# Mixture-of-experts layers of a two-layer decoder: two token lists in separate expert tiles, or in shared ones

## The chip, the cores and the metric

The kernel runs on one core of a Trainium2 chip, as one launch. The metric is the device time of that launch in microseconds, the median of several runs. The profiled executions are single ones, taken by the hardware profiler.

## The reference

A pre-layernorm decoder of two layers over x of 64 x 64 tokens (4096) of width 128, all in fp32. Each layer adds to x a sequence mixer, a cross-attention over a context of 64 tokens, and a feed-forward part with 8 routed experts (128 to 512 to 128), of which each token uses 2:

```python
# layer 0: sigmoid gate, two shared experts, exact gelu
balanced = sigmoid(x @ centroids.T + routing_bias)
_, top_idx = top_k(balanced, 2)
top_w = softmax(take_along_axis(sigmoid(raw), top_idx, -1), -1)
h_r = gelu(einsum('bsd,efd->bsef', x, Wfc_r)); expert_out = einsum('bsef,edf->bsed', h_r, Wproj_r)
return x + shared_out + einsum('bsed,bse->bsd', expert_out, combine)
# layer 1: softmax gate, biases, tanh gelu
topk_scores, topk_idx = top_k(softmax(x @ Wg + bg), 2)
for e in range(8):
    output = output + (gelu(x @ W1[e] + b1[e]) @ W2[e] + b2[e]) * combine_w[..., e:e + 1]
```

The change touches these two parts alone.

## The kernel before

The program is a row of phases: state-space mixer, attention, `ffn0`, retention, attention, `ffn1`. Both feed-forward phases are `ffn_phase` with other settings. The names below are those of its code.

**Routing.** The 4096 tokens are 32 token tiles of 128, in 8 groups of 4. DVE normalizes x (`xn`), TensorE makes the gate's logits, and DVE turns them into one-hots of the first and second expert. Two products (`prefix`) give, for each token, how many tokens of its tile stand before it at its expert, and each tile's count by expert. From these a chain of DVE instructions, each of which waits for the one before (`seq`), works out for every token and choice a slot: a place in a list ordered by expert and padded so that each expert begins a new *expert tile* of 128 slots.

**Two lists.** The token tiles are cut in two parts of 20 and 12 (`part_tiles`). Each part has its own list with its own padding: 2 x 20 x 128 + 8 x 127 slots cut to whole tiles is 47 expert tiles, and 31 for the second. These are fixed lengths, so M = 78 tiles are computed whatever the routing is. The first list is ready sooner, so that the tiles can start; the one-hots of the last three groups (`hot`) are made inside the loop at steps 4, 10 and 16.

**From slot to token.** `hot` makes, for a group, one-hots of the slot's row and of its tile; `collect` multiplies them on TensorE (16 products with 47 or 31 columns), and the sum in PSUM is the token of each slot. `sources` copies it to `source`. In `ffn1` POOL makes one of the two multiplications of `hot` for the first five groups (`BY_POOL`). The expert of each tile (`owner`) comes from eight DVE instructions on one partition, four for each list.

**The tile loop.** For each tile POOL gathers 128 rows of `xn` by an indirect DMA; TensorE transposes them, DVE copies the transpose, ACT copies the expert's up weights, TensorE makes 4 up products (8 instructions), ACT the gelu (with DVE's bias before it in `ffn1`), TensorE 4 down products (8 instructions), DVE copies the result out, and SP stores each two tiles to DRAM (`slots_y`). Step s transposes tile s, does the up products of tile s - 2 and the down products of tile s - 4. POOL issues the gathers in lots of up to 4 tiles; a lot waits until TensorE has transposed a tile that is 8 to 20 before its end (`AHEAD_FIRST`, `AHEAD_MORE`).

**Back to tokens.** After the last lot POOL gathers, for each group, the two result rows of each token: 8 indirect DMAs a group. Groups 0 to 4 wait for the first list's stores, 5 to 7 for all. The rows go to two buffers (those of `hot_row`), so the turn for group m waits until DVE has added group m - 2 to x (`add_rows`). DVE adds group 0 from step 72 on in `ffn0`, groups 0 and 1 from steps 66 and 72 in `ffn1`, a quarter in each step, and the others after the loop.

**Around the loops.** In `ffn0` two shared experts work on all tokens in 16 units on TensorE: 6 units before the loop, with `prefix` and the `collect`s between them, 10 after it. In `ffn1` there are none. TensorE fills the waits with transposes whose result nobody reads (`warm`: 28 at the phase's start, 88 after `prefix`, 6 after each `collect`, 24 more).

Of the kernel before, what the change touches and what calls it, by code (L numbers as in the profile page):

```python
# [19 lines left out]
F32 = mybir.dt.float32  # L20
# [3 lines left out]
ALU = mybir.AluOpType  # L24
# [1403 lines left out]
def ffn_phase(g, name, spec):  # L1428
# [6 lines left out]
    parts, E, PM = len(part_tiles), E0 + EXPERTS, max(part_tiles)  # L1435
    V = parts * EXPERTS
    counts = [slot_tiles(t) for t in part_tiles]
    M, NM = sum(counts), max(counts)
    start = [sum(counts[:part]) for part in range(parts + 1)]
    first_tile = [sum(part_tiles[:part]) for part in range(parts + 1)]  # L1440
    first_group = [t // GTILES for t in first_tile]
    part_of = [part for part in range(parts) for _ in range(counts[part])]
    RING = TILES
    BY_POOL, ADDED_AT = range(first_group[1]) if spec["last"] else (), spec["added_at"]
    lots = [(start[part] + begin, size) for part in range(parts)
            for begin, size in in_lots(counts[part], (1, 1, 2, 4) if part == 0 else (4,))]
    lot_of = {begin: n for n, (begin, _) in enumerate(lots)}
    stores = [(part, begin, size) for part in range(parts) for begin, size in in_lots(counts[part], (STORED,))]
    store_of = {start[part] + begin + t: n for n, (part, begin, size) in enumerate(stores) for t in range(size)}
    stores_of = [sum(1 for part, _, _ in stores if part < upto) for upto in range(parts + 1)]  # L1450
    with ExitStack() as ctx:
# [12 lines left out]
        if biased:  # L1464
# [3 lines left out]
        slots_y = [nc.dram_tensor(f"{name}_slots_y{part}", (counts[part] * P, D), F32,  # L1468
                                  kind="Internal").ap() for part in range(parts)]

        by_token, by_expert = [P, TILES, EXPERTS], [P, V, PM]
# [13 lines left out]
        tile_starts, tile_numbers = sb("tile_starts", [P, TILES]), sb("tile_numbers", [P, NM])  # L1485
# [4 lines left out]
        ones_row, per_tile, running, over = (lent(k, by_expert) for k in ("ones_row", "per_tile", "running", "over"))  # L1490
        earlier, count, tiles = sb("earlier", [P, V]), sb("count", [P, V]), sb("tiles", [P, V])
        tile_end, offset = sb("tile_end", [P, V]), sb("offset", [P, V])
        ended, tile_owner = lent("ended", [1, NM, EXPERTS]), sb("tile_owner", [1, NM])
# [76 lines left out]
        with nc.Block() as block:  # L1570
# [26 lines left out]
            def _(pool):  # L1597
# [28 lines left out]
                for m in range(GROUPS):  # L1626
                    part = max(p for p in range(parts) if first_group[p] <= m)
                    if m in first_group:
                        stores_done(pool, stores_of[part + 1])
# [10 lines left out]
            def _(dve):  # L1640
# [127 lines left out]
                for q in range(first_group[1]):  # L1768
                    hot(q)
# [326 lines left out]
```

## Time and profile before

| | us |
|---|---|
| median of 3 runs | 1282.48 |
| the three runs | 1277.87, 1282.48, 1283.58 |
| profiled execution, whole | 1278.75 |
| its span, first to last instruction | 1277.0 |
| TensorE matmuls busy | 1135.2 (89%) |
| DVE busy | 830.1 (65%) |
| ACT busy | 652.2 (51%) |
| POOL busy | 611.2 (48%) |
| mean granted TensorE clock | 0.95 |

Times in the profile count from the first instruction. `ffn0` runs from 208 to 516 us, its loop from 284.7 to 441.1; `ffn1` from 1008 to the end, its loop from 1064.1 to 1223.9. PE is TensorE, PEld its weight loads, DVE VectorE, ACT ScalarE, POOL GpSimd, SP the engine that issues plain DMAs. In a timeline a row says when a run of like instructions starts, how long it takes, how many they are, and in brackets how long the engine had been idle before it and what ended that. The end of a row is its start plus its length.

### The profile page before, as it was taken

The numbers are of one execution on the slowest core, as the hardware profiler recorded it, in microseconds if no ns is written. First come the engines' busy times: TensorE is split into PE (matmuls) and PEld (weight loads), VectorE is DVE, ScalarE is ACT, GpSimd is POOL, SyncE is SP. The second block draws the span as 40 slices with busy tenths as digits, with TensorE's granted clock in tenths as the row PEclk, the third lists the DMA queues.
The fourth block names the chain that finished last, engine by engine and source line by source line (L and its number), as shares of the span: only waits on it lengthen the run. The fifth ranks groups of instructions, "written<-read, shape, count | busy, mean of one in ns | idle before, by whom it ended". The sixth has DMA issues, their size and how long they took to land. (4 is left out here: it accounts for less than half of the span.)

```text
span 1277.0 us, 31999 instructions
## 1 busy us (share of the span) xinstructions
PE 1135.2 (89%) x11702; PEld 959.3 (75%) x11702; DVE 830.1 (65%) x1800; ACT 652.2 (51%) x1171; POOL 611.2 (48%) x627
## 2 busy tenths in 40 slices
PE   6979997999999999399999999987899878999930
PEld 4766666689999877288888888875577778999930
DVE  6868997743222343378888888884689675666742
ACT  5417774425566542166665665653687503566610
POOL 4761325126567474733334444333254326566775
PEclk9999999899999999699999999998999888999975
DMA  7001213202233321100000000000110331233332
GB/s 193 10 2 49 54 49 136 102 17 65 71 77 82 98 71 32 39 2 1 0 0 0 1 0 0 0 1 6 21 19 17 113 109 44 68 79 78 87 108 64
DMA packets 61908, 62.64 MB, mean 49 GB/s; under 512 B 12592, under 2 KB 50864, under 8 KB 61296
## 3 DMA queue, kind: packets, MB, share of 16 engines
q1 hardware_dynamic: 51824, 42.52, 11.2%
q0 software_dynamic: 9088, 18.63, 6.3%
q8 instruction: 62, 1.02, 0.3%
q14 instruction: 38, 0.31, 0.1%
q10 hardware_dynamic: 896, 0.17, 0.1%
HBM read 42.67 MB, written 16.52 MB: 46 GB/s over the span
## 5 line engine op out<-in xcount | busy, mean ns | idle before, releaser
L1623 POOL DMA_INDIRECT f_xn<-f_xn_rows,f_source x156 | 149.0, 955 | 49.4 <-issue 48.2
L1977 PE MATMUL f_bank<-f_xT,f_w_tile 128*128 128x128 f32 x1248 | 167.5, 278 | 0.0
L1988 PE MATMUL f_bank<-f_w_down,f_hidden 128*128 x1248 | 165.1, 276 | 0.0
L1977 PEld LDWEIGHTS f_bank<-f_xT,f_w_tile 128*128 128x128 f32 x1248 | 154.4, 195 | 0.0
L1988 PEld LDWEIGHTS f_bank<-f_w_down,f_hidden 128*128 128x128 f32 x1248 | 152.5, 193 | 0.0
L1634 POOL DMA_INDIRECT f_hot_row<-f_slots_y,f_slots x128 | 123.7, 966 | 38.3 <-issue 38.0
L1050 POOL TENSOR_TENSOR ret_rstd<-ret_var,ret_minus_half 128x8 f32<-128x8 f32 x32 | 52.7, 1647 | 173.8 <-DVE ret_var L1089 173.8
L1879 ACT ACTIVATE f_w_tile<-f_w_up 128x512 f32 x156 | 96.3, 620 | 30.1 <-DVE f_owner L1778 28.3
L885 PEld LDWEIGHTS a_mixed_psum<-a_v_diag,a_probT 128*64 128x64 f32 x2048 | 66.6, 139 | 59.9 <-ACT a_probT L837 43.7
L747 POOL TENSOR_TENSOR X<-X,a_mixed 128x128 f32<-128x128 f32 x64 | 29.2, 456 | 159.2 <-DVE a_mixed L780 155.8
L788 DVE TENSOR_REDUCE a_top<-a_scores 128x16 f32<-128x1024 f32 x64 | 78.3, 1224 | 36.0 <-PE a_scores L870 34.8
L837 ACT ACTIVATE a_probT<-a_probT_psum 128x1024 f32<-128x1024 f32 x64 | 65.5, 1024 | 57.8 <-PE a_probT_psum L896 57.8
L1828 DVE COPY f_y_out<-f_bank 128x128 f32<-128x128 f32 x78 | 22.6, 290 | 102.0 <-PE f_bank L1988 102.0
L1053 POOL TENSOR_TENSOR ret_qk<-ret_qk,ret_turned 128x1024 f32<-128x1024 f32 x32 | 76.3, 2387 | 25.1 <-DVE ret_turned L1109 25.0
L1889 ACT ACTIVATE f_hidden<-f_before_gelu 128x512 f32<-128x512 f32 x78 | 49.1, 630 | 71.6 <-DVE f_before_gelu L1813 71.5
L1889 ACT ACTIVATE f_hidden<-f_bank 128x512 f32<-128x512 f32 x78 | 46.6, 597 | 68.9 <-PE f_bank L1977 68.9
L791 DVE TENSOR_TENSOR a_prob<-a_scores,a_top 128x1024 f32<-128x1024 f32 x64 | 78.3, 1224 | 2.2
L885 PE MATMUL a_mixed_psum<-a_v_diag,a_probT 128*64 128x18 f32 x2048 | 72.0, 213 | 7.9 <-ACT a_probT L837 5.9
L896 PE MATMUL a_probT_psum<-ident,a_prob 128*128 128x128 f32 x512 | 70.5, 281 | 5.9 <-ACT a_prob L811 5.9
L1398 ACT ACTIVATE f_s_hidden<-f_bank 128x512 f32<-128x512 f32 x64 | 38.2, 597 | 65.2 <-PE f_bank L1372 65.2
L1258 PE MATMUL ret_ps<-ret_wo,ret_gated 128*128 128x128 f32 x512 | 67.1, 285 | 4.9 <-DVE ret_gated L1081 4.8
L811 ACT ACTIVATE a_prob<-a_prob 128x1024 f32<-128x1024 f32 x64 | 67.1, 1049 | 6.2 <-DVE a_shift L764 3.3
(284 smaller groups left out, 2788.1 us busy)
## 6 DMA issues: line engine op xcount, KB each, us to landing
f_slots_y<-f_y_out SPq DMA_DIRECT2D x76, 128.0 KB, 2.0
a_v_rows<-in_ctx SPq DMA_DIRECT2D x16, 256.0 KB, 4.0
f_xn_rows<-f_xn SPq DMA_DIRECT2D x16, 256.0 KB
f_w_up<-in_f_up SPq DMA_DIRECT2D x1, 2560.0 KB, 10.2
f_w_down<-in_f_down SPq DMA_DIRECT2D x1, 2560.0 KB, 17.7
f_xn<-f_xn_rows,f_source POOLq DMA_INDIRECT x156, 2.6
X<-in_x SPq DMA_DIRECT2D x4, 512.0 KB, 7.6
kv_ctxT<-in_ctxT SPq DMA_DIRECT2D x8, 256.0 KB, 5.9
```

The costliest lines, as they stand in the source:

```text
L788: dve.tensor_reduce(top[b][:], bank_s[b][:], AXIS.X, ALU.max).then_inc(S["top_ready"], 1)
L791: dve.tensor_tensor(prob[b][:], bank_s[b][:], top[b][:].unsqueeze(2).to_broadcast([P, HEADS, SEQ]), ALU.subtract)\
L811: nc.scalar.activation(prob[b][:], prob[b][:], ACT.Exp, scale=1.0 / math.sqrt(HEAD))\
L885: last = pe.matmul(bank_o[64 * row:64 * row + 64, 18 * hp:18 * hp + 18], probT[b][:, hp, 64 * row:64 * row + 64], v_diag[octet][:, 2 * (tu ...
L896: last = pe.transpose(bank_t[:, hp, :], prob[b][:, 2 * hp:2 * hp + 2, :].rearrange("p h t -> p (h t)"), g.ident[:])
L1053: pool.tensor_tensor(qk[k % 2][:], qk[k % 2][:], turned[k % 2][:], ALU.add)\
L1623: pool.indirect_dma_start(out=x_in[:, s % RING, :], out_offset=None, in_=xn_rows[:, :], in_offset=bass.IndirectOffsetOnAxis(ap=source[:, s ...
L1634: pool.indirect_dma_start(out=rows[m % 2][:, t, n, :], out_offset=None, in_=slots_y[part][:, :], in_offset=bass.IndirectOffsetOnAxis(ap=sl ...
L1879: nc.scalar.activation(w_tile[s % W_RING][:].unsqueeze(1), w_up[:, bass.ds(expert + E0, 1), :], ACT.Copy)\
L1889: nc.scalar.activation(hidden[m % 3][:].rearrange("p j t -> p (j t)"), before_gelu[m % 3][:].rearrange("p j t -> p (j t)") if biased else ...
L1977: last = pe.matmul(bank_h[m % 3][:, j * P:(j + 1) * P], w_tile[m % W_RING][:, j * P:(j + 1) * P], xT[m % 3][:], start=True, stop=True)
L1988: last = pe.matmul(bank_y[m % 2][:, 0:D].unsqueeze(1), hidden[m % 3][:, j, :], w_down[:, bass.ds(expert + E0, 1), j, :], start=(j == 0), s ...
```

## The change

The two lists share expert tiles. Each expert now has one stretch of slots for both parts; the tiles are ordered in three *segments*: those that the first part fills wholly, those in which the parts may meet, and those of the second part. So the padding is paid once: (2 x 32 x 128 + 1016) / 128 = 71 tiles. `early` = 33 tiles are sure to hold tokens of the first part alone; `whole` = 48 tiles may hold some. The first five groups' products have columns 0 to 48, the later ones' 33 to 71, and the 15 columns that both touch are kept in `mixed` and added. Lots beyond tile 33 wait for the second list. The owners come from one column on 128 partitions and one product with the identity on TensorE. The additions begin at steps 65 (`ffn0`) and 60 and 66 (`ffn1`). There is one constant load more, `segment_table`. `more_rows` is 0, so the row buffers stay two.

```diff
-    parts, E, PM = len(part_tiles), E0 + EXPERTS, max(part_tiles)
-    counts = [slot_tiles(t) for t in part_tiles]
-    M, NM = sum(counts), max(counts)
+    M, SEGMENTS = slot_tiles(TILES), parts + 1
+    early = (TOP_K * part_tiles[0] * P - EXPERTS * (P - 1) + P - 1) // P
+    whole = [TOP_K * sum(part_tiles[:part + 1]) + EXPERTS for part in range(parts - 1)] + [M]
+    columns = [(0, whole[0]), (early, M)]
...
-                 (rank[:], dram["rank"]), (before[:], dram["before"]), (tile_starts[:], dram["tile_starts"]),
+                 (rank[:], dram["rank"]), (before[:], dram["before"]), (tile_bounds[:], dram["tile_bounds"][:, 3 - parts:3, :]),
-                 (tile_numbers[:], dram["tile_numbers"][:, 0:NM]), (row_numbers[:], dram["row_numbers"]),
+                 (tile_numbers[:], dram["tile_numbers"]), (segment_table[:], dram["segment_table"]), (row_numbers[:], dram["row_numbers"]),
...
-                    waits = [(S["source_ready"], part_of[begin] + 1), (S["xT_in_psum"], begin + size - AHEAD_FIRST - AHEAD_MORE * begin // M)]
+                    waits = [(S["source_ready"], 1 if begin + size <= early else 2), (S["xT_in_psum"], begin + size - AHEAD_FIRST - AHEAD_MORE * begin // M)]
...
-                        stores_done(pool, stores_of[part + 1])
-                    turn(pool, (added[1], GTILES * (m - 1)), (S["hot_used"], GROUPS))
+                        stores_done(pool, stores_for[part])
+                    turn(pool, (added[1], GTILES * (m - len(rows) + 1)), (S["hot_used"], GROUPS))
...
+                seq(dve.tensor_copy(per_tile[:], bank_c.rearrange("p t e -> p e t")))
+                seq(dve.tensor_copy(before_it[:, 1:EXPERTS], running[:, 0:EXPERTS - 1, TILES - 1]))
+                seq(dve.tensor_tensor(count[:], running[:, :, part_tiles[0] - 1::part_tiles[1]],
+                                      before_it[:].unsqueeze(2).to_broadcast(per_count), ALU.subtract))
+                shape = [P, EXPERTS, parts, TILES]
+                seq(dve.tensor_tensor(over[:], count[:].unsqueeze(3).to_broadcast(shape),
+                                      tile_bounds[:].unsqueeze(1).to_broadcast(shape), ALU.is_gt))
+                seq(dve.tensor_reduce(full[:].rearrange("p k e -> p e k"), over[:], AXIS.X, ALU.add))
+                seq(dve.tensor_copy(until[:, 1::parts, :], full[:, 0::parts - 1, :]))
+                seq(dve.scalar_tensor_tensor(out=until[:, 2:parts + 1, :], ..., op0=ALU.add, op1=ALU.min))
+                seq(dve.tensor_tensor(tiles[:], until[:, 1:, :], until[:, 0:SEGMENTS, :], ALU.subtract))
+                seq(dve.tensor_tensor_scan(flat(tile_end), flat(ones_row)[:, 0:SEGMENTS * EXPERTS], flat(tiles), 0.0,
+                                           ALU.mult, ALU.add))
+                seq(dve.tensor_tensor(shift[:], tile_end[:], until[:, 1:, :], ALU.subtract))
+                seq(dve.scalar_tensor_tensor(out=first_shift[:], ...))
+                seq(dve.tensor_tensor(more[:], shift[:, 1:, :], shift[:, 0:parts, :], ALU.subtract))
+                seq(dve.scalar_tensor_tensor(out=limit[:], ...))
+                seq(dve.tensor_tensor(logit[:], bank_p, running[:].rearrange("p e t -> p t e"), ALU.add))
                 for part in range(parts):
+                    seq(dve.tensor_tensor(key[:, at, :], logit[:, at, :], limit..., ALU.is_ge))
+                    seq(dve.tensor_tensor(key[:, at, :], key[:, at, :], more..., ALU.mult))
+                    seq(dve.tensor_tensor(logit[:, at, :], logit[:, at, :], first_shift..., ALU.add))
+                seq(dve.scalar_tensor_tensor(out=logit[:], in0=key[:], scalar=float(P), in1=logit[:],
+                                             op0=ALU.mult, op1=ALU.add))
...
+                def sources_first():
+                    dve.wait_ge(S["hot_used"], front)
+                    dve.tensor_copy(source[:, 0:early], bank_s[0][:, 0:early]).then_inc(S["source_ready"], 1)
+                    seq(dve.tensor_copy(mixed[:], bank_s[0][:, early:whole[0]]))
+                def sources_rest():
+                    dve.wait_ge(S["hot_used"], GROUPS)
+                    seq(dve.tensor_tensor(source[:, early:whole[0]], bank_s[1][:, 0:whole[0] - early], mixed[:], ALU.add))
+                    dve.tensor_copy(source[:, whole[0]:M], bank_s[1][:, whole[0] - early:M - early])\
+                        .then_inc(S["source_ready"], 1)
...
-                sources(0)
-                for part in range(parts):
-                    ... (four instructions on one partition for each list)
+                seq(dve.scalar_tensor_tensor(out=ended[:], in0=flat(tile_end), scalar=segment_table[:, 4 * EXPERTS:],
+                                             in1=segment_table[:, 0:SEGMENTS * EXPERTS], op0=ALU.is_le, op1=ALU.mult))
+                dve.tensor_reduce(tile_owner[:], ended[:], AXIS.X, ALU.add).then_inc(S["owner_column"], 1)
+                sources_first()
+                dve.wait_ge(S["owner_in_psum"], 1)
+                dve.tensor_scalar(owner[:], bank_o, float(EXPERTS - 1), None, ALU.min).then_inc(S["owner_ready"], 1)
...
+                def owners():
+                    pe.wait_ge(S["owner_column"], 1)
+                    pe.matmul(bank_o, tile_owner[:], g.ident[:, 0:M], start=True, stop=True)\
+                        .then_inc(S["owner_in_psum"], 1)
...
+                        if place == (5, "up"):
+                            owners()
...
                         warm(WARM_BETWEEN)
+                    owners()
                     warm(WARM_UP)
...
-    ffn_phase(g, "f0", dict(..., added_at=(72,), ...))
+    ffn_phase(g, "f0", dict(..., added_at=(65,), hot_later=(4, 10, 16), listed=16, ahead=(8, 13), more_rows=0, ...))
-    ffn_phase(g, "f1", dict(..., added_at=(66, 72), ...))
+    ffn_phase(g, "f1", dict(..., added_at=(60, 66), hot_later=(4, 10, 16), listed=16, ahead=(8, 13), more_rows=0, ...))
```

## Rows read from the trace of the kernel before

**Rows 1.** Busy time by stage: start:end, each engine busy us (instructions), clock, DMA, GB/s
```profile
284.70:441.10 156.40, 154.28 (x1377) 153.46 (x1376) 46.61 (x174) 88.48 (x153) 92.63 (x114) 1.00 0.30 72
...
441.10:516.10 75.00, 70.19 (x402) 50.87 (x400) 32.43 (x100) 26.71 (x43) 42.82 (x47) 0.99 0.21 62
...
1064.10:1223.90 159.80, 157.69 (x1372) 156.66 (x1372) 106.65 (x260) 88.21 (x153) 102.73 (x126) 0.98 0.30 74
...
1223.90:1277.00 53.10, 0.00 (x0) 0.00 (x0) 13.68 (x49) 0.00 (x0) 33.06 (x38) 0.54 0.31 87
```

**Rows 2.** Timeline of TensorE, first loop: start us, us, engine, line, operation, [idle before]
```profile
323.85 0.27 PE L1968 MATMUL f_bank<-ident,f_xn 128*128 128x128 f32 x1
...
433.81 0.27 PE L1968 MATMUL f_bank<-ident,f_xn 128*128 128x128 f32 x1
```

**Rows 3.** Timeline of SP and of TensorE, first feed-forward, loads and their wait
```profile
212.66 0.43 SPq L1539 DMA_DIRECT2D f_w_down<-in_f_down  x1
...
230.41 9.47 PE L1372 MATMUL f_bank<-f_xnT,f_w_up 128*128 128x512 f32 x16 [1.10 <-DMA f_w_down<-in_f_down]
```

**Rows 4.** Timeline of DVE, second feed-forward, routing chain
```profile
1032.52 0.62 DVE L1699 COPY f_per_tile<-f_bank 128x160 f32<-128x160 f32 x2 [1.90 <-issue]
1033.17 0.82 DVE L1702 TENSOR_TENSOR_SCAN f_running<-f_ones_row,f_per_tile 128x320 f32<-128x320 f32 x1
...
1034.23 0.18 DVE L1705 TENSOR_TENSOR f_count<-f_running,f_earlier 128x16 f32<-128x16 f32 x1
...
1038.11 0.26 DVE L1726 TENSOR_TENSOR f_logit<-f_logit,f_offset 128x96 f32<-128x96 f32 x1
1038.40 0.42 DVE L1675 TENSOR_TENSOR f_key<-f_logit,f_first 128x256 f32<-128x256 f32 x1
```

**Rows 5.** Timeline of DVE and of TensorE, first feed-forward, first one-hots
```profile
251.45 0.69 DVE L1407 TENSOR_TENSOR X<-f_bank,X 128x512 f32<-128x512 f32 x1 [1.66 <-PE f_bank L1385]
...
253.10 1.22 DVE L1752 TENSOR_TENSOR f_hot_row<-f_row_numbers,f_row_of 128x1024 f32<-128x1024 f32 x1
...
254.59 1.88 PE L1936 MATMUL f_bank<-f_hot_tile,f_hot_row 128*128 128x47 f32 x16
```

**Rows 6.** Timeline of TensorE, first loop, product with a later group's one-hots
```profile
292.55 1.97 PE L1936 MATMUL f_bank<-f_hot_tile,f_hot_row 128*128 128x31 f32 x16 [0.40 <-DVE f_hot_row L1752]
```

**Rows 7.** Timeline of TensorE, second feed-forward, ahead of its loop
```profile
1008.12 5.81 PE L1902 MATMUL f_bank<-ident 128*128 128x128 f32 x28 [2.24 <-PEq L109]
...
1044.08 1.96 PE L1936 MATMUL f_bank<-f_hot_tile,f_hot_row 128*128 128x47 f32 x16 [1.28 <-POOL f_hot_tile L1613]
...
1055.43 3.47 PE L1902 MATMUL f_bank<-ident 128*128 128x128 f32 x30
...
1064.13 0.45 PE L1968 MATMUL f_bank<-ident,f_xn 128*128 128x128 f32 x1 [3.10 <-DVE f_xT L1808]
```

**Rows 8.** Timeline of DVE, second feed-forward, around the owners
```profile
1055.64 0.21 DVE L1759 CAST f_source<-f_bank 128x47 int32<-128x47 f32 x1 [3.10 <-PE f_bank L1936]
...
1058.87 0.42 DVE L1785 TENSOR_REDUCE f_rec<-f_score 128x32 f32<-128x256 f32 x1
```

**Rows 9.** Busy time by slice of 4 us around the second loop's start
```profile
1060.00:1064.00 4.00, 0.33 (x1) 0.14 (x1) 3.06 (x10) 2.29 (x3) 3.22 (x5) 0.65 0.18 55
1064.00:1068.00 4.00, 3.87 (x18) 3.83 (x18) 1.47 (x4) 0.82 (x2) 3.23 (x5) 0.50 0.18 51
```

**Rows 10.** Timeline of POOL, end of the second feed-forward
```profile
1174.73 0.19 POOL L1424 TENSOR_TENSOR f_turn_cell<-ident 128x1 f32<-128x1 f32 x1 [2.24 <-PE f_bank L1968]
...
1204.10 0.20 POOL L1424 TENSOR_TENSOR f_turn_cell<-ident 128x1 f32<-128x1 f32 x1
...
1215.35 0.19 POOL L1424 TENSOR_TENSOR f_turn_cell<-ident 128x1 f32<-128x1 f32 x1 [1.03 <-issue]
...
1226.31 0.19 POOL L1424 TENSOR_TENSOR f_turn_cell<-ident 128x1 f32<-128x1 f32 x1 [0.49 <-issue]
```

**Rows 11.** The page's DMA issues: operation, count, KB each, median us to landing
```profile
f_slots_y<-f_y_out SPq DMA_DIRECT2D x76, 128.0 KB, 2.0
```

More of the change, by code:

```diff
@@ L1489, in ffn_phase @@
         top, rec = sb("top", [P, TILES]), sb("rec", [P, TILES])
[L1490 to L1493, printed above, removed]
+        ones_row, per_tile, running = (lent(k, by_expert) for k in ("ones_row", "per_tile", "running"))
+        over = lent("over", [P, EXPERTS, parts, TILES])
+        count, full = sb("count", [P, EXPERTS, parts]), sb("full", [P, parts, EXPERTS])
+        until, before_it = sb("until", [P, SEGMENTS + 1, EXPERTS]), sb("before_it", [P, EXPERTS])
+        tiles, tile_end, shift = (sb(k, [P, SEGMENTS, EXPERTS]) for k in ("tiles", "tile_end", "shift"))
+        first_shift, limit, more = (sb(k, [P, parts, EXPERTS]) for k in ("first_shift", "limit", "more"))
+        ended, tile_owner = sb("ended", [P, SEGMENTS * EXPERTS]), sb("tile_owner", [P, 1])
+        mixed = sb("mixed", [P, whole[0] - early])
         row_of, tile_of = (sb(k, [P, TOP_K, TILES]) for k in ("row_of", "tile_of"))
@@ L1708, in _ @@
-                seq(dve.tensor_reduce(tiles[:], over[:], AXIS.X, ALU.add))
-                seq(dve.tensor_tensor_scan(tile_end[:], flat(ones_row)[:, 0:V], tiles[:], 0.0, ALU.mult, ALU.add))
-                for part in range(parts - 1, 0, -1):
-                    before_it = part * EXPERTS
-                    seq(dve.tensor_scalar(tile_end[:, experts_of(part)], tile_end[:, experts_of(part)],
-                                          tile_end[:, before_it - 1:before_it], None, ALU.subtract))
@@ L1718, in _ @@
+                seq(dve.scalar_tensor_tensor(out=first_shift[:], in0=shift[:, 0:parts, :], scalar=float(P),
+                                             in1=before_it[:].unsqueeze(1).to_broadcast(per_part),
                                              op0=ALU.mult, op1=ALU.subtract))
+                seq(dve.tensor_tensor(more[:], shift[:, 1:, :], shift[:, 0:parts, :], ALU.subtract))
+                seq(dve.scalar_tensor_tensor(out=limit[:], in0=until[:, 1:parts + 1, :], scalar=float(P),
+                                             in1=before_it[:].unsqueeze(1).to_broadcast(per_part),
+                                             op0=ALU.mult, op1=ALU.add))
@@ L1741, in hot @@
                     need(dve, S["hot_used"], q - 1)
-                    N = counts[max(p for p in range(parts) if first_group[p] <= q)]
-                    shape, out = [P, TOP_K, GTILES, N], hot_tile[b][:, :, :, 0:N]
-                    dve.tensor_tensor(out, tile_numbers[:, 0:N].unsqueeze(1).unsqueeze(1).to_broadcast(shape),
+                    begin, end = columns[q >= front]
+                    shape, out = [P, TOP_K, GTILES, end - begin], hot_tile[b][:, :, :, 0:end - begin]
+                    dve.tensor_tensor(out, tile_numbers[:, begin:end].unsqueeze(1).unsqueeze(1).to_broadcast(shape),
                                       tile_of[:, :, at].unsqueeze(3).to_broadcast(shape), ALU.is_equal)\
@@ L1820, in _ @@
                         n = store_of[m]
[L1821 removed]
+                        at = m - stores[n][0]
                         if at == 0:
```

158 lines of the change are left out of this document (75 added, 83 removed).

## The prediction

> **What bounds the kernel now.** I read the stage table first [rows 1]. Four stages belong to the two feed-forward phases. In the first tile loop (284.7 to 441.1 us) TensorE is busy 154.28 of 156.40 us at full clock; in the second 157.69 of 159.80. So both loops go by TensorE. The 75 us after the first loop are TensorE's too (70.19 busy): ten units of shared experts, beside which the row gathers run. The last 53.1 us have no TensorE work at all: POOL issues row gathers, 33.06 us busy and the rest issue time between them. The loops' pace comes from two transposes of the first loop [rows 2]: from tile 19 at 323.85 to tile 77 at 433.81 there are 58 tiles, 109.96 / 58 = 1.896 us each.
>
> **The tiles.** The lengths are fixed by a formula, not by the data. Before: (2 x 20 x 128 + 1016) / 128 = 47 and (2 x 12 x 128 + 1016) / 128 = 31, 78 in all. After: (2 x 32 x 128 + 1016) / 128 = 71. Seven tiles fewer in each of two loops is 7 x 1.896 = 13.3 us each, -26.5 together. Every padded tile costs a full one, so this doesn't hang on the routing. The rest of the change gives some of it back, and each loop has its own end, so I take the phases apart.
>
> **First feed-forward, entry.** There is one more constant load ahead of the two weight loads on SP. The w_down row shows that an issue holds the queue 0.43 us, and TensorE stands still 1.10 us until w_down lands [rows 3]. One issue more is +0.45 (bounds 0 and 0.6: the loads share the engines, so some may be made good). DVE's chain meets TensorE again at the counts, so both shift.
> Then the routing chain on DVE grows. I price it with the same operations of the second phase [rows 4]; the next one starts 0.03 to 0.04 after each. A 16-element step costs 0.22, 96 elements 0.29, 256 elements 0.46 (so some 1.0 ns an element, and 160 elements 0.36), the scan over 320 0.86. Removed, up to the product with the first one-hot: 1032.52 to 1038.40, 5.88 us. New: one copy of 256 out of PSUM 0.50, scan over 256 0.73, then `over` and its reduce, each of 512 elements, at 0.72 each (0.46 + 256 x 1.0 ns), ten small ones (before_it, count, two for until, tiles, tile_end, shift, first_shift, more, limit) 10 x 0.22 = 2.2, running minus per_tile 0.46, the sum out of PSUM 0.50, three of 160 at 0.36, three of 96 at 0.29, and one of 256 at 0.46. Sum 8.2, so +2.35 us (bounds 1.8 and 3.0, by the price of the wide ones).
> In the first phase shared experts run on TensorE meanwhile. DVE idled 1.66 us ahead of the shared sum at 251.45, waiting for TensorE; of the 2.35 that wait hides 1.66, and 0.7 appears. The one-hot rows of group 0 were finished at 253.10 + 1.22 = 254.32, and TensorE began its product with them at 254.59 [rows 5], a cover of 0.27. That leaves 0.4; a semaphore's way and what the wait had of slack I can't read, so I take 0.6 (0 to 1.2). Groups 1 to 4 are behind waits on TensorE's own products, so nothing more comes. The owner product, one weight load and 71 columns, is +0.2 here (0 to 0.5). Behind DVE's new wait for it stand the owner copy, the weights' normalization and the shared sum of group 1, and all have over 3 us until TensorE needs them.
>
> **In both loops.** The three later groups make one-hot tiles of 38 columns in place of 31: 304 elements against 248, two instructions, 2 x 56 x 1.0 ns = 0.11 us each time. TensorE already waits 0.40 for these [rows 6], so 3 x 0.11 = +0.35 per loop (0 to 1.0; the second instruction in the last listing, 0.25, lies beside TensorE's next tile). Expert lots from tile 32 on now need the second list, which is there at step 17; their gather is not due until tile 23 has been transposed: 6 tiles or 11 us of cover.
>
> **First feed-forward, end.** The gathers are released by tile numbers, with 20 to 22 tiles to go in both versions, and the first additions begin 6 tiles from the end in both. TensorE runs on with the shared experts, so the end moves with the loop: -13.3 + 0.45 + 0.6 + 0.2 + 0.35 = **-11.7**.
>
> **Second feed-forward, entry.** Here nothing covers the routing: TensorE spins on 88 idle transposes and had already waited 1.28 us for the first one-hots [rows 7]. The 2.35 us count in full. But owners come sooner. Before, between the source copy at 1055.64 and the weights' normalization at 1058.87 [rows 8], DVE made eight owner instructions on one partition. Now two small ones stand ahead of the source copy, where DVE idles 3.10 us, and behind it come the copy of `mixed` 0.2, the wait for the product (TensorE is in six idle transposes, about 0.7 long, then the product) and one owner copy 0.25: about 1.2 in place of 3.2, so -2.0 (bounds -2.4 and -0.5, the latter if the product is queued behind slow transposes). DVE's x copy released TensorE at 1064.13, after 3.10 us of idling [rows 7], so this counts in full. Net +0.35; the extra load issue is hidden by the 28 idle transposes at the start, which end at 1008.12 + 5.81 = 1013.9 [rows 7].
>
> **The clock.** The gap before the first collection grows from 1.28 to 3.6 us. Ahead of the loop TensorE is nearly idle from 1055.43 + 3.47 = 1058.9 on, and the granted clock is 0.65 in the slice 1060 to 1064 and 0.50, the lower level of 1.2 GHz, in the next [rows 9], after gaps of which the last was 3.10. So I take a fall in the new gap of 3.6 too. In the slow slice 18 instructions took 3.87 us, 0.215 each, against 1.896 / 17 = 0.112. With the lower level for 2 to 4 us the collection loses 1 to 2 us: I take +1.5 (0 to 3). The shorter gap ahead of the loop could in turn spare the slow start of it, up to -1.8; I take 0. The Trainium skill (TensorE: Matmul & The Clock Gate, "Why this matters for your kernels") asks to avoid long idle gaps between bursts because the gate goes back to the low rate. By that rule the sum is the one below; without it, 1.5 less. The trace agrees: 0.50 after the gap that ends at 1064.13.
>
> **Second feed-forward, end.** It is POOL's chain of row gathers, released lot by lot by transposed tiles: the lot before the last at tile 56 of 78, at 1174.73 [rows 10]. After, it is tile 49 of 71. So the chain moves with the loop, -13.3. But two additions come one step nearer to the end: they stood 12 and 6 tiles before it (66 and 72 of 78) and now 11 and 5 (60 and 66 of 71). POOL's turn at 1204.10 had no wait and would get one of 1.9; the turn at 1215.35 waits for the additions of group 1 and comes 1.9 later; the turn at 1226.31 waited 0.49 for additions behind the loop's end and no longer would: 1215.35 + 1.9 + 10.5 = 1227.7 in old time against 1226.31 + 0.3 of restart. So +1.1 at the end (0 to 2). Row gathers of the first list need 48 tiles stored; with a landing of 2.0 us [rows 11] that comes up to 1 us after POOL is ready, and it vanishes in the 1.9 before the next turn. Sum: -13.3 + 0.35 + 0.35 + 1.5 + 1.1 = **-10.0**.
>
> **Sum.** -11.7 - 10.0 = -21.7. The profiled execution took 1278.75 (span 1277.0), so 1257.0 on its footing. It lies at the low end of the three runs, 3.7 below their median of 1282.48; on the median's footing it is 1260.8. The three differ by 5.7 us, so I forecast 1258.5.
>
> **Rivals.**
> *B, the clock doesn't fall in the new gap, or the shorter gap ahead of the loop spares the slow start:* -21.7 - 1.5 - 1.8 = -25.0, 1255. For it: behind the gap of 1.28 the 16 products took 1.96 us, fast, and ahead of the loop two gaps had added up. Against: the slice 1060 to 1064. 20%.
> *C, half of the gain is lost at the end:* POOL's chain is set by something else than the transposes, so the second phase's end hardly moves: -11.7 and some, 1268. For it: POOL's gathers are eight groups of over 10 us in a row, and they now depend on 48 tiles of 71 stored where 47 of 78 were needed. Against: by the landing row that is 1 us late, not ten. 12%.
> *D, slower than before:* the second loop falls to the lower clock level and stays there, because its first tiles wait for DVE. By the slow slice a tile costs 17 x (0.215 - 0.112) = 1.75 us more. From 12 to 13 such tiles on (21.7 / 1.75) the change loses; at 20 it is +13, 1292. For it: the loop of before starts slow. Against: the second loop's mean clock is 0.98, and by 1080 it has settled. 3%.
> *E, it doesn't do what it says:* some longer wait of the second list cancels the gain, about 1280. The tile count is static, so 3%.
> The forecast itself has 62%.
>
> **How the numbers follow.** 1258.5 is the forecast's. B to most of C gives 1252 to 1268. What a measurement can tell from no change is about 0.5%, 6 us: faster is forecast, B and C, 94%; within it 3%; slower 3%.
>
> **What would show each step.** Tile pace 1.896 unchanged and 71 transposes per loop. First phase: TensorE's wait for w_down near 1.5, a wait of some 0.5 for group 0's one-hots. Second phase: 8.2 us from the per_tile copy to the product with the first one-hot in place of 5.88, idling of some 3.6 ahead of the first collection with a granted clock below 1 behind it, the weights' normalization about 1.2 after the source copy, waits of 2.3 ahead of the collections in the loops no longer than 0.52, a POOL wait of nearly 3 us ahead of the gathers of group 3. I am wrong if the loops' pace changes, if TensorE waits for gathers inside a loop, or if the last 53 us grow by more than 2.

## The result and the profile after

| | before | after |
|---|---|---|
| median, us | 1278.70 (5 runs) | 1269.79 (5 runs) |
| lowest to highest | 1277.87 to 1283.58 | 1267.04 to 1271.76 |
| profiled execution, its span | 1277.0 | 1268.0 |
| mean granted TensorE clock | 0.950 | 0.937 |

After over before is 0.9915, 95% interval 0.9892 to 0.9938: 8.9 us faster by the medians and 10.9 by the ratio, where 20 to 24 were forecast. The time lies 1.8 us above the top of the range that I gave (1252 to 1268). The sign was right, the size half.

The stretches compared below lie between marks that both traces have: the start of the retention phase, the idle transposes at the start of the second feed-forward, the first collection, the source copy, and chosen transposes of the loop.

*First feed-forward.* The retention phase's first product starts at 512.19 in place of 522.50: -10.3. The timeline of TensorE in the first phase after the change (start us, us, engine, line, operation; in brackets the idle time before it and what ended it):

```profile
230.04 9.65 PE L1372 MATMUL f_bank<-f_xnT,f_w_up 128*128 128x512 f32 x16 [0.70 <-DMA f_w_down<-in_f_down]
...
254.99 1.99 PE L1963 MATMUL f_bank<-f_hot_tile,f_hot_row 128*128 128x48 f32 x16 [0.42 <-DVE f_hot_row L1776]
...
269.18 5.43 PE L1385 MATMUL f_bank<-f_w_down,f_s_hidden 128*128 128x128 f32 x32
...
279.76 0.28 PE L1969 MATMUL f_bank<-ident,f_tile_owner 128*1 128x71 f32 x2
...
295.22 1.98 PE L1963 MATMUL f_bank<-f_hot_tile,f_hot_row 128*128 128x38 f32 x16 [0.52 <-DVE f_hot_row L1776]
...
324.82 0.31 PE L2003 MATMUL f_bank<-ident,f_xn 128*128 128x128 f32 x1
...
423.44 0.27 PE L2003 MATMUL f_bank<-ident,f_xn 128*128 128x128 f32 x1
```

The wait for `w_down` is 0.70, less than the 1.10 of [rows 3]. Group 0's one-hots are late by a stall of 0.42, the owner product is 0.28, the waits in the loop 0.52 against 0.40 of [rows 6]. The pace is unchanged: 98.62 us for 52 tiles, 1.897 each. One row doesn't follow from the change, the one at 269.18: 32 products that took 3.73 at 240.39 take 5.43 here. The granted clock falls to 0.50 in the middle of busy work and is back at 1.00 some 3.5 us later.

*Second feed-forward.* It took 268.88 us from its first idle transpose to the end before (1008.12 to 1277.0), and 270.34 after (997.66 to 1268.0): with seven tiles fewer, 1.5 us **more**. TensorE ahead of its loop:

```profile
1036.42 2.85 PE L1963 MATMUL f_bank<-f_hot_tile,f_hot_row 128*128 128x48 f32 x16 [3.79 <-POOL f_hot_tile L1620]
1039.07 1.51 PE L1927 MATMUL f_bank<-ident 128*128 128x128 f32 x6
1040.37 3.49 PE L1963 MATMUL f_bank<-f_hot_tile,f_hot_row 128*128 128x48 f32 x16
...
1054.13 3.49 PE L1963 MATMUL f_bank<-f_hot_tile,f_hot_row 128*128 128x48 f32 x16
...
1058.85 0.40 PE L1969 MATMUL f_bank<-ident,f_tile_owner 128*1 128x71 f32 x2
1059.18 3.79 PE L1927 MATMUL f_bank<-ident 128*128 128x128 f32 x24
1062.80 0.38 PE L2003 MATMUL f_bank<-ident,f_xn 128*128 128x128 f32 x2
1064.87 0.33 PE L2003 MATMUL f_bank<-ident,f_xn 128*128 128x128 f32 x1 [1.69 <-DMA f_xn<-f_xn_rows,f_source]
...
1069.99 0.33 PE L2003 MATMUL f_bank<-ident,f_xn 128*128 128x128 f32 x1 [2.89 <-DMA f_xn<-f_xn_rows,f_source]
```

And the same stretch by slices of 4 us (start:end, length, busy us and instructions of TensorE, its weight loads, DVE, ACT and POOL, granted clock, DMA share, GB/s):

```profile
1038.00:1042.00 4.00, 4.00 (x21) 4.00 (x21) 1.70 (x2) 0.00 (x0) 2.25 (x2) 0.50 0.00 0
...
1054.00:1058.00 4.00, 4.00 (x21) 4.00 (x20) 0.27 (x2) 0.00 (x0) 0.07 (x1) 0.50 0.00 0
1058.00:1062.00 4.00, 4.00 (x24) 3.43 (x23) 2.47 (x7) 1.91 (x4) 3.49 (x6) 0.60 0.11 35
1062.00:1066.00 4.00, 2.31 (x21) 2.08 (x20) 2.37 (x9) 1.06 (x1) 3.10 (x5) 1.00 0.16 49
```

The gap ahead of the first collection grew from 1.28 [rows 7] to 3.79. Behind it the clock falls to its lower level of 1.2 GHz and stays there for the collections: 21 instructions in each full slice, where two full slices of the kernel before hold 39 and 38. The first collection takes 2.85 in place of 1.96, the other four 3.49 in place of 1.88. From the first collection to the source copy it is 21.23 us (1036.42 to 1057.65) in place of 11.56 (1044.08 [rows 7] to 1055.64 [rows 8]): **+9.67**.

The stretches of the second phase add up to its +1.5: the gate +0.4, the routing chain +2.4, the collections +9.7, source copy to fifth transpose -0.4 (12.34 in place of 12.72), from there to the 19th, with the three later collections, +1.25, the rest of the loop -13.3, the tail +1.4. In the +1.25 stands another short fall of the clock, some 2.4 us behind a wait of 0.70:

```profile
1092.00:1094.00 2.00, 2.00 (x12) 2.00 (x11) 0.69 (x1) 0.24 (x1) 1.30 (x2) 0.50 0.03 8
```

From the 13th to the 15th transpose it is 5.45 us (1091.27 to 1096.72) in place of 3.83, so this fall cost 1.6; without it the stretch would have been no longer than before.

### The profile page after: what moved, and what is told of

Read it like the earlier page. It is cut to its first block and busy times, and to the rows that moved or that the text cites. A ratio compares the mean times of both kernels' runs of the same rounds, so it can differ in the third digit from the quotient of the medians.

```text
span 1268.0 us, 31262 instructions
## 1 busy us (share of the span) xinstructions
PE 1124.9 (89%) x11468; PEld 947.8 (75%) x11468; DVE 820.4 (65%) x1773; ACT 635.4 (50%) x1143; POOL 595.8 (47%) x609
## 5 line engine op out<-in xcount | busy, mean ns | idle before, releaser
L1630 POOL DMA_INDIRECT f_xn<-f_xn_rows,f_source x142 | 136.3, 960 | 45.2 <-issue 45.0
L2012 PE MATMUL f_bank<-f_xT,f_w_tile 128*128 128x128 f32 x1136 | 151.7, 277 | 0.0
L2023 PE MATMUL f_bank<-f_w_down,f_hidden 128*128 x1136 | 151.1, 277 | 0.0
L2012 PEld LDWEIGHTS f_bank<-f_xT,f_w_tile 128*128 128x128 f32 x1136 | 139.9, 194 | 0.0
L2023 PEld LDWEIGHTS f_bank<-f_w_down,f_hidden 128*128 128x128 f32 x1136 | 139.6, 194 | 0.0
L1904 ACT ACTIVATE f_w_tile<-f_w_up 128x512 f32 x142 | 87.7, 620 | 41.0 <-DVE f_owner L1806 39.1
L1914 ACT ACTIVATE f_hidden<-f_before_gelu 128x512 f32<-128x512 f32 x71 | 44.7, 630 | 68.6 <-DVE f_before_gelu L1839 68.6
L1914 ACT ACTIVATE f_hidden<-f_bank 128x512 f32<-128x512 f32 x71 | 42.4, 597 | 64.9 <-PE f_bank L2012 64.9
```

The source lines that it names most:

```text
L1630: pool.indirect_dma_start(out=x_in[:, s % RING, :], out_offset=None, in_=xn_rows[:, :], in_offset=bass.IndirectOffsetOnAxis(ap=source[:, s ...
L1904: nc.scalar.activation(w_tile[s % W_RING][:].unsqueeze(1), w_up[:, bass.ds(expert + E0, 1), :], ACT.Copy)\
L1914: nc.scalar.activation(hidden[m % 3][:].rearrange("p j t -> p (j t)"), before_gelu[m % 3][:].rearrange("p j t -> p (j t)") if biased else ...
L2012: last = pe.matmul(bank_h[m % 3][:, j * P:(j + 1) * P], w_tile[m % W_RING][:, j * P:(j + 1) * P], xT[m % 3][:], start=True, stop=True)
L2023: last = pe.matmul(bank_y[m % 2][:, 0:D].unsqueeze(1), hidden[m % 3][:, j, :], w_down[:, bass.ds(expert + E0, 1), j, :], start=(j == 0), s ...
```

## Experiments

All were run beside the kernel before on the same chip; the ratio is to it. WARM_COUNT is the number of idle transposes between `prefix` and the first collection in the second phase.

**1. The gap closed (after).**

```diff
-WARM_START, WARM_COUNT, WARM_BETWEEN, WARM_UP = 28, 88, 6, 24
+WARM_START, WARM_COUNT, WARM_BETWEEN, WARM_UP = 28, 112, 6, 24
```

> The changed kernel with 112 idle transposes after the count products in place of 88; nothing of the computation differs. Theory (gap): in the second feed-forward the longer routing chain leaves TensorE idle 3.79 us ahead of the first collection, the clock falls to 1.2 GHz there, and it stays there for the whole collection, which took 21.2 us against 11.6. 24 transposes at 0.11 us close the gap to some 1.2 us; the collection takes 11.6 us again and the launch gets 9 to 10 us shorter, about 1260. Rival (products): the collection is slow because of what it multiplies (48 columns, another order of sums), whatever the gap; then the collection stays at 21 us and the launch at 1269. Rival (forecast's size): a fall costs 1 to 3 us and the rest was lost elsewhere; then about 1267.

1259.52 us (1258.67 to 1262.69), ratio 0.9843 (0.9830 to 0.9857), against 0.9915 without. In its trace the gap is 1.11 and the collections are back at 1.88:

```profile
1038.37 1.96 PE L1963 MATMUL f_bank<-f_hot_tile,f_hot_row 128*128 128x48 f32 x16 [1.11 <-POOL f_hot_tile L1620]
...
1048.01 1.88 PE L1963 MATMUL f_bank<-f_hot_tile,f_hot_row 128*128 128x48 f32 x16
```

24 idle transposes give back 9 to 10 us: nearly the whole of what was missing.

**2. The gap opened (before).** The same edit the other way on the kernel before, 88 to 64.

> The kernel before with 64 idle transposes after the count products in place of 88. The gap ahead of the first collection grows from 1.28 to some 3.9 us, and nothing else changes. Theory (gap): the clock falls, the collection takes 21 us in place of 11.6, the launch gets 9 to 10 us longer, about 1288. Rival (products): the products of before, with 47 columns, stay fast; no change, 1279. Rival (forecast's size): 1280 to 1282.

1290.51 us (1288.61 to 1290.67), ratio 1.0078 (1.0064 to 1.0092). The gap is 3.90, the first 47-column collection takes 3.60 and the other four 3.49 each, at a granted clock of 0.50:

```profile
1047.13 3.60 PE L1936 MATMUL f_bank<-f_hot_tile,f_hot_row 128*128 128x47 f32 x16 [3.90 <-POOL f_hot_tile L1613]
...
1051.83 3.49 PE L1936 MATMUL f_bank<-f_hot_tile,f_hot_row 128*128 128x47 f32 x16
```

```profile
1048.00:1052.00 4.00, 4.00 (x21) 4.00 (x21) 1.76 (x3) 0.00 (x0) 1.80 (x2) 0.50 0.00 0
```

So neither 48 columns nor the new routing makes the collections slow; the gap alone costs the kernel before 10 us.

**3 and 4. One phase at a time.** The change in `ffn0` only, and in `ffn1` only. Both are the kernel after with one phase put back: `ffn_phase_lists` is the `ffn_phase` of the kernel before. First the edit of number 3, then that of number 4:

```diff
-    ffn_phase(g, "f1", dict(..., added_at=(60, 66), ...))
+    ffn_phase_lists(g, "f1", dict(..., added_at=(66, 72), ...))
...
-    ffn_phase(g, "f0", dict(..., added_at=(65,), ...))
+    ffn_phase_lists(g, "f0", dict(..., added_at=(72,), ...))
```

> The change in the first feed-forward alone; the second has its two separate lists (47 + 31 tiles). Theory: the first phase carries nearly all of the measured gain, 10.3 us by the two traces, because its routing lies beside shared experts: about 1268.5. Forecast on record: -11.7. Rival: the gain comes from both phases evenly, then -4.5.

> The change in the second feed-forward alone; the first has its two separate lists. Theory: seven tiles saved, and all given back at the collection: by the two traces +1.4 us, about 1280. Forecast on record: -10.0, 1269. Rival (evenly): -4.5.

First phase alone 1268.19 us (ratio 0.9911, 0.9895 to 0.9927), second alone 1279.58 (0.9999, 0.9987 to 1.0010). All that the change gives comes from the first phase. The traces say how much. From the first idle transpose of the first feed-forward to the first product of the retention phase it is 313.99 to 315.51 us in the four kernels with the old first phase (mean 314.6), and 300.66 to 303.70 in the nine with the new one (mean 302.4): **-12.2**. The starts of the second phase agree: 1008.12, 1010.77, 1011.16 and 1011.90 (mean 1010.5), and 993.70 (experiment 5) and 997.66 to 1000.39 (the other eight), mean 998.4.

**5. Idle transposes behind the gap, in place of before it (after).**

```diff
                     if q in BY_POOL:
                         pe.wait_ge(S["hot_tile_ready"], q + 1)
+                    if q == 0 and not shared:
+                        warm(32)
```

> The kernel after, with 32 transposes of 128 columns between the wait for the first one-hots of the second feed-forward and its first collection (48 columns). Theory (what the engine does decides: narrow products behind the fall keep the clock low, wide ones bring it back): the clock falls in the 3.8 us gap as before, rises during the 32 transposes (they take 5 to 6 us in place of 3.8), and the five collections take 1.9 us each in place of 3.5, so that source copy comes 5.5 us later for the transposes and 9.7 earlier for the clock: about 1265.5 (1264 to 1267). Rival (the clock comes back some 20 us after the gap, whatever the engine does): the collections still take 3.5 us each for at least 15 us, and the transposes are added on top: about 1275.

1265.90 us (1259.24 to 1267.96, 6 runs), ratio 0.9893 (0.9875 to 0.9910). The profiled execution was the fastest, 1259.24:

```profile
1032.45 5.35 PE L1927 MATMUL f_bank<-ident 128*128 128x128 f32 x32 [3.74 <-POOL f_hot_tile L1620]
1037.63 1.88 PE L1965 MATMUL f_bank<-f_hot_tile,f_hot_row 128*128 128x48 f32 x16
```

The time is the expected one (1264 to 1267), so the rival with 1275 is out. The gap is still 3.74, the clock falls and is low for most of the 32 transposes, and 5.2 us later the first collection runs at 1.88. In the kernel after, the same 5.2 us behind the gap TensorE was as busy, with collections and six transposes behind each, and another 17 us of them brought no rise. The profiled execution is not a typical one: the other five lie 5 to 9 us above it. Its second phase began at 993.70, 5.2 us before the mean of the other eight kernels with the new first phase, so most of that lead was won ahead of the edit. Its second phase took 263.7 us, against 270.34 in the kernel after and 260.4 in the first experiment.

**6. The owners alone (before).** Two lists kept; the owner code of the change put in:

```diff
-                sources(0)
-                for part in range(parts):
-                    ... (four instructions on one partition for each list)
+                seq(dve.tensor_tensor(ended..., tile_end[:], tile_numbers[:, NM:NM + 1]..., ALU.is_le))
+                dve.tensor_reduce(tile_owner[:], ended[:], AXIS.X, ALU.add).then_inc(S["owner_column"], 1)
+                sources(0)
+                dve.wait_ge(S["owner_in_psum"], 1)
+                dve.tensor_scalar(owner[:], bank_o, float(EXPERTS - 1), None, ALU.min).then_inc(S["owner_ready"], 1)
```

> The kernel before, both lists kept, only the owners made in the new way: one comparison and one reduction on 128 partitions ahead of the source copy, two products with the identity on TensorE (47 and 31 columns), one owner copy. Theory (owners stood on the path to the second loop alone): weights' normalization 1.3 to 1.9 us after the source copy in place of 3.2, the first up products as much earlier, the second loop shifted by it, nothing in the first phase: -1.4 us, ratio 0.999 (-2.0 by the forecast's term). Rival (the gathered rows, not the weights' normalization, release the second loop): ratio 1.000, the gap ahead of the third transpose is then put down to the gathers. Second rival: the shorter gap spares the slow start of the loop: -3, ratio 0.9975.

1281.65 us (12 runs), ratio 1.0010 (0.9998 to 1.0022): nothing, as the first rival has it. DVE did get free sooner: the weights' normalization starts at 1060.45, 1.05 after the source copy at 1059.40, in place of 3.23 [rows 8]. But TensorE then waits for rows:

```profile
1062.87 0.27 PE L1973 MATMUL f_bank<-ident,f_xn 128*128 128x128 f32 x1
1064.14 0.33 PE L1973 MATMUL f_bank<-ident,f_xn 128*128 128x128 f32 x1 [1.00 <-DMA f_xn<-f_xn_rows,f_source]
1066.77 0.33 PE L1973 MATMUL f_bank<-ident,f_xn 128*128 128x128 f32 x1 [2.30 <-DMA f_xn<-f_xn_rows,f_source]
...
1071.82 0.48 PE L1973 MATMUL f_bank<-ident,f_xn 128*128 128x128 f32 x1 [2.82 <-DMA f_xn<-f_xn_rows,f_source]
```

From the source copy to the fifth transpose it is 12.42 here, 12.72 before, 12.34 after. In the first experiment it is 12.53. It is nearly the same each time. The fifth tile is the first of a lot of four, so POOL has to issue eight gathers first; here they run from 1059.68 to 1070.25 without a wait, whatever DVE and TensorE do.

**7. TensorE's idling ahead of the loop filled (after).**

```diff
-WARM_START, WARM_COUNT, WARM_BETWEEN, WARM_UP = 28, 88, 6, 24
+WARM_START, WARM_COUNT, WARM_BETWEEN, WARM_UP = 28, 112, 6, 44
```

> The kernel after with 112 idle transposes behind the prefix products (as in the earlier run) and 44 in place of 24 behind the owner product: they fill TensorE's idling ahead of the second loop, where the clock fell to 0.5 for some 10 us. Theory (a long idle gap costs the clock, idle work of full width beside it is free): the extra 20 end at about 1055.8 where the third transpose waits until 1057.3 for its rows anyway; the clock stays at 1.0 until then and the first up products take 1.06 us in place of 1.9; the next gather (tile 4) still paces the start, so -1.7 us against 112 alone (0 to -4): 1257.8. Rival (the gathers alone set the loop's entry): the products are faster but the waits for the gathers grow by as much: 1259.5. Second rival (the transposes delay the first two of the loop and so the chain): +2, 1261.5.

1260.95 us, ratio 0.9853 (0.9836 to 0.9871): as the first experiment, so the first rival holds. The products do run faster, the first up products 1.06 in place of 1.92, and the wait ahead of the fifth transpose grows from 1.02 to 2.87. The gathers set the entry; the lower clock there costs nothing.

**8. The tail: gathers of xn sooner (after, with 112).**

```diff
-    ... hot_later=(4, 10, 16), listed=16, ahead=(8, 13) ...
+    ... hot_later=(4, 10, 16), listed=16, ahead=(8, 20) ...
```

> The kernel after with 112 idle transposes and, in the second feed-forward, the gathers of xn released up to 28 tiles ahead in place of 21 (AHEAD_MORE 20 in place of 13), so POOL ends them some 10 us earlier. Theory (the end of the second phase now hangs on the store of the 48th tile, which POOL waits for before its first gather of result rows): POOL's turn for group 0 stays at 1168 and so does the end: 1259.5, same as with 112 alone. Rival (the forecast's: the chain at the end is released by transposed tiles, so the gathers of xn set it): the turn for group 0 comes up to 10 us earlier and the end 3 to 10 us earlier, 1250 to 1256.

1260.12 us, ratio 0.9837 (0.9818 to 0.9855), no change from 0.9843. POOL's turn for group 0, first in the kernel after, then in this one:

```profile
1175.79 0.19 POOL L1424 TENSOR_TENSOR f_turn_cell<-ident 128x1 f32<-128x1 f32 x1 [2.27 <-DMA f_slots_y<-f_y_out]
...
1206.85 0.19 POOL L1424 TENSOR_TENSOR f_turn_cell<-ident 128x1 f32<-128x1 f32 x1 [0.56 <-issue]
...
1247.72 0.20 POOL L1424 TENSOR_TENSOR f_turn_cell<-ident 128x1 f32<-128x1 f32 x1
```

```profile
1150.43 0.21 POOL L1424 TENSOR_TENSOR f_turn_cell<-ident 128x1 f32<-128x1 f32 x1
...
1166.90 0.19 POOL L1424 TENSOR_TENSOR f_turn_cell<-ident 128x1 f32<-128x1 f32 x1 [12.66 <-DMA f_slots_y<-f_y_out]
```

The wait for the 48th tile's store was 2.89 in the first experiment, the fair comparison, and is 12.66 here: the ten microseconds that POOL wins on the gathers of xn turn into waiting. Counted from the phase's start, the turn for group 0 comes 2.1 us sooner (166.5 against 168.6), and waits of 0.81 and 1.00 ahead of the turns for groups 2 and 3 take that back; the phase takes 260.4 us in both. The store of the first list starts the tail, not the lots.

**9 and 10. A shorter first list.** If the tail is eight turns of 10.2 us from that store on, the first list has to be stored earlier. Number 9:

```diff
-    part_tiles=(20, 12), ... added_at=(60, 66), hot_later=(4, 10, 16), listed=16, ahead=(8, 13), more_rows=0
+    part_tiles=(16, 8, 8), ... added_at=(56, 61, 67), hot_later=(2, 6, 10, 14), listed=14, ahead=(8, 22), more_rows=1
```

with 128 and 44 idle transposes. Number 10 has `part_tiles=(16, 16)` with 112 and 44, and otherwise the same settings. Both change several things at once against the first experiment (parts, release of the gathers, buffers, additions), so their gain isn't divided among these.

> The kernel after with 128 and 44 idle transposes, and in the second feed-forward three parts of 16, 8 and 8 token tiles in place of two of 20 and 12 (groups 0 to 3 need 40 stored tiles, 4 and 5 need 56, the last two all 71), the later one-hots at steps 2, 6, 10 and 14, the gathers of xn up to 30 tiles ahead, a third buffer for result rows, additions from steps 56, 61 and 67. Theory (the end of the second phase is POOL's row of eight turns of 10.3 us, which starts when the list of group 0 is stored): 8 tiles fewer are 15 us earlier, so the turn for group 0 comes at about 1154 in place of 1167 to 1168, the others follow back to back, the last at about 1227, and the end 20 us behind it; the third part adds some 2 us of DVE's chain ahead of the loop: 1249 (1247 to 1253). Rival (the end goes by the last stores and the additions behind the loop): groups 6 and 7 wait for them whatever stands before, and the time stays at 1258 to 1261. Second rival (the later entry of the second list starves the loop from tile 25 on): waits for gathers inside the loop, above 1262.

> As the run with three parts, but two parts of 16 and 16 token tiles, and 112 idle transposes: groups 0 to 3 need 40 stored tiles, groups 4 to 7 all 71. Theory (turns back to back from the stored list on): the turn for group 0 at 1154, the first four done by 1195, then POOL waits for the last store at about 1205; the last turn at 1236 and the end at 1257, so the time is 1257 (1255 to 1259), some 8 above the version with three parts and 2 to 3 below two parts of 20 and 12 (1260). Rival (the last stores do not bound the turns): within 2 us of the version with three parts.

Three parts: 1253.78 us (1250.00 to 1254.51), ratio 0.9789 (0.9769 to 0.9809). Halves: 1258.29 (1254.47 to 1262.50), 0.9828 (0.9803 to 0.9854). They stand in the order that the theory gives, number 9 0.8 us above its range. The difference is 4.5, not 8, because the collections were slow in number 9; against experiment 11, where they are fast as in number 10, it is 9.6. With halves POOL waits 11.37 us for the last stores between its fourth and fifth turn (the row names DVE's additions, but those that this turn needs were done at 1188.35; the last product of the loop ends at 1204.24, and its store is what comes 2 us later):

```profile
1155.06 0.21 POOL L1424 TENSOR_TENSOR f_turn_cell<-ident 128x1 f32<-128x1 f32 x1
...
1206.82 0.19 POOL L1424 TENSOR_TENSOR f_turn_cell<-ident 128x1 f32<-128x1 f32 x1 [11.37 <-DVE X L1568]
```

With three parts the turns run from 1161.39 to 1232.19 without a wait, 10.1 each. They start 7 us later than I expected. What holds POOL now is the second list: it waits 13.71 us for DVE's second source copy, which comes after the product at step 14, and from there issues without a pause.

```profile
1101.34 0.19 POOL L1424 TENSOR_TENSOR f_turn_cell<-ident 128x1 f32<-128x1 f32 x1 [13.71 <-DVE f_source L1790]
...
1161.39 0.20 POOL L1424 TENSOR_TENSOR f_turn_cell<-ident 128x1 f32<-128x1 f32 x1
```

In experiments 10 and 11 this wait is 13.72 and ends at 1095.04 and 1095.63, and the turn for group 0 comes at 1155.06 and 1155.66, near the 1154 that I expected. So nearly 6 of the 7 us are the slow collections ahead of the loop, which made both lists late. They were slow again in this execution, behind a gap of only 0.95, and from the second on:

```profile
1038.10 1.95 PE L1963 MATMUL f_bank<-f_hot_tile,f_hot_row 128*128 128x40 f32 x16 [0.95 <-POOL f_hot_tile L1620]
...
1040.57 3.13 PE L1963 MATMUL f_bank<-f_hot_tile,f_hot_row 128*128 128x40 f32 x16
...
1049.40 3.48 PE L1963 MATMUL f_bank<-f_hot_tile,f_hot_row 128*128 128x40 f32 x16
```

**11. No gap at all.** Number 9 with 144 idle transposes in place of 128.

> The version with three parts, with 144 in place of 128 idle transposes behind the prefix products. With 128 a gap of 0.95 us was left ahead of the first collection, and in the profiled execution the clock fell to 0.50 in the second collection and stayed there until the 44 wide transposes. The 16 more take 1.8 us, close the gap and delay the first collection by 0.9. Theory (the gap ahead of narrow products is what makes the clock fall): no fall, five rows of collections at 1.88 us, the entry 4 to 5 us shorter less 0.9: 1250 (1248 to 1252). Rival (collections of 40 and 48 columns can lose the clock without any gap): the collections are at 0.50 again in the profile, and the time is 1254 to 1255.

**1248.70 us** (1247.15 to 1251.10), ratio 0.9761 (0.9742 to 0.9780). It is the fastest version of this study: 31 us below the kernel before, some 20 below the change as it stood. The granted clock is 0.951 or 0.952 in all five executions, against 0.944 to 0.947 in the five of experiment 9. All collections take 1.88:

```profile
1023.04 16.70 PE L1927 MATMUL f_bank<-ident 128*128 128x128 f32 x144
1039.58 1.88 PE L1963 MATMUL f_bank<-f_hot_tile,f_hot_row 128*128 128x40 f32 x16
...
1046.77 1.88 PE L1963 MATMUL f_bank<-f_hot_tile,f_hot_row 128*128 128x40 f32 x16
```

Counted from the phase's first idle transpose (997.66 and 998.51), the 16 transposes delay the first collection by 0.6 us, and they are worth 5.

## Why the prediction was right in sign and twice too large in size

- *The tiles, -13.3 a loop:* right. Pace 1.897, and -13.27 from the 19th transpose to the last, in both loops.
- *First phase, -11.7:* -10.3 in the profiled pair, -12.2 between the means over thirteen traces. The term for the added load (+0.45) had the wrong sign in this pair, the wait for `w_down` became 0.4 shorter. The late one-hots (+0.6, measured 0.42) and the in-loop waits (0.52 foreseen and measured) were right. The 1.7 us that the clock's fall at 269.18 cost are most of the difference between the two figures. Experiment 4, whose first phase is the old one, has such a fall too (granted 0.72 and 0.50 from 268 to 272), and experiment 3, with the new first phase, has none, so the change is neither needed for it nor enough.
- *Routing chain, 8.2 us in place of 5.88:* measured 8.30, from 1022.42 to 1030.72:

```profile
1022.42 0.42 DVE L1703 COPY f_per_tile<-f_bank 128x256 f32<-128x256 f32 x1 [1.91 <-issue]
...
1024.02 0.69 DVE L1712 TENSOR_TENSOR f_over<-f_count,f_tile_bounds 128x512 f32<-128x512 f32 x1
...
1026.98 0.17 DVE L1735 SCALAR_TENSOR_TENSOR f_limit<-f_until,f_before_it 128x16 f32<-128x16 f32 x1
...
1030.72 0.42 DVE L1682 TENSOR_TENSOR f_key<-f_logit,f_first 128x256 f32<-128x256 f32 x1
```

- *The clock, +1.5 (0 to 3):* **this is the step that failed.** It cost 9.7. I foresaw the gap (3.6, measured 3.79) and the fall, and then gave the lower level "2 to 4 us". The slice of [rows 9] gave no ground for a recovery within the collections; I took the quick one at the loop's start as the rule. The price to work out as the upper bound was all five collections at the lower level: their pitch is 4.59 there (1044.95 to 1049.54) and 2.39 at full clock, and 5 x 2.2 is 11.0; the first was partly fast, so 9.7 came of it. With 11.0 in place of 1.5 the sum would have been -12.2, which is 1266.5 on the profiled execution's footing and 1268.0 on the forecast's. The Trainium skill (TensorE: Matmul & The Clock Gate, "What's actually happening") says that the default is throttled and that activity releases it. Here the first half agrees: the granted clock is 0.50 from 1018 to 1020, in a wait of 6.13 us ahead of the prefix products. The second half is not enough: TensorE was busy 4.00 of 4.00 us in five slices in a row at a granted clock of 0.50. Ahead of the loop the clock rose each time within a long row of idle transposes (here, and in experiments 2, 5 and 9).
- *Owners, -2.0:* failed as well. DVE's part of it was right in kind (3.23 became 1.86, and 1.05 in experiment 6), but the wait that took its place, for POOL's first eight gathers, leaves 0.4 of it. I read who released TensorE at 1064.13 [rows 7] and did not ask what stood next behind it.
- *Tail, +1.1:* measured +1.4, by another mechanism. I said that the store of the 48th tile comes 1 us late and vanishes in the next wait. It came 2.27 late, and what shrank was the wait before group 3's turn, 0.56 in place of the nearly 3 that I named. Experiment 8 shows that this store starts the tail.
- *The rivals.* B (no fall) is what experiment 1 made: 1259.5 where I had said 1255. C had the right time, 1268, and named the wrong place: the end of the second phase moved by 1.4 only; the loss is at its entry. D, a whole loop at the lower level, did not happen. But its mechanism did, ahead of the loop.

By terms, the second phase missed by 11.5: the clock 8.2, the owners 1.6, the loop from the fifth to the 19th transpose 0.9 (the short fall at 1092 alone cost 1.6), the rest 0.8.

## What to carry to other kernels

A step on DVE that makes TensorE wait costs its own length. If the clock falls, it also costs the slowing of all the work that follows until the clock rises (here 3.49 us a collection in place of 1.88): price a fall as the whole next stretch at the lower clock. Where idle transposes bridge a wait, their number belongs to the length of that wait; whoever lengthens the chain beside them has to lengthen them too (here 24 more were worth 9 to 10 us, and 16 more in the version with three parts were worth 5). And when a wait is shortened, look for the next one behind it before counting the gain: both the owners and the earlier gathers bought only another wait.

## What the runs showed of the hardware that I had not expected

- The granted clock stayed at 0.50 for 20 us and more with TensorE busy all the time on products of 48 columns with a weight load each and six transposes behind every 16, and rose within the next 24 transposes (1059.18, 3.79 us). In experiment 5 it rose within the 32 transposes that followed the fall at once (1032.45, 5.35 us).
- A fall can come behind the gap: in the kernel after, the granted clock is 1.00 through the whole gap and in the slice 1036 to 1037, and 0.63 from 1037 to 1038. Ahead of the second loop of the kernel before it had fallen by the gap's end (0.65 in the slice 1060 to 1064 [rows 9]).
- It can fall without a gap of note: at 269 to 273 us in the first phase, amid busy work, in the kernel after (and likewise in experiments 1 and 4, but not in the others), at 1092 in its second loop, 2.4 us behind a wait of 0.70, and 3 us behind a gap of 0.95 us in experiment 9, where a like gap of 0.99 in experiment 10 left it at 1.00 through the collections ahead of the loop. What makes the difference between executions stays open.
- POOL issues row gathers at 10.1 to 10.2 us a group of eight wherever nothing holds it, with TensorE's loop and the stores beside them (experiment 9, from 1161) or without.
